# Moving a batch's projections up into the phase before, and finishing the last tokens tile by tile

## The chip, the cores and the metric

The kernel runs on one core of a Trainium2 chip. The metric is the device time in microseconds (us) of one execution; lower is better.

## The reference

Two layers on `x` of 4 batches, 512 tokens and 256 channels in float32, with a layer norm after each residual sum:

```python
x = layernorm(x + linear_attention(x))   # 16 heads of 128, elu(q)+1 and elu(k)+1, 4 key heads
x = layernorm(x + gated_update(x))       # 8 experts, the one with the largest gate, rank 8
x = layernorm(x + softmax_attention(x))  # 16 heads of 16, queries and keys from this x ("x2")
x = layernorm(x + top2_experts(x))       # 8 experts of 32, two by score, and a rank-16 part
```

In the softmax attention `q = x @ Wq`, `k = x @ Wk`, `v = x @ Wv`, and `softmax(q k / 4) v @ Wo` is taken per batch and head. In the expert layer the hidden vector (3 x 128 numbers for each token) is multiplied by a down matrix and added to `x`.

## The kernel before

Each engine has its own hand-written order of work; they meet only at semaphores. Tokens are cut into four tiles of 128 (`NT = 4`), the channels into two halves (`KD = 2`). Products that need accuracy are made in three passes of split numbers (`_hi` and `_lo`), so most results come as a pair: ScalarE (ACT) copies the `_hi` part out of PSUM, VectorE (DVE) subtracts to get the `_lo` part.

**First phase** (`layer0_attention`). Four batches, one after the other. For each, after keys and values, a run over 16 queries (`query(b, n)`), and then a run of 16 `project(b, n)`, which add into `bank_y`. Each project needs its head scaled: TensorE (PE) broadcasts a factor (`factor`), DVE multiplies (`scale`), ACT copies (`scaled_hi`), and the low part comes from DVE for even n and from GpSimd (POOL) for odd n (`scaled_lo`, lines 628 and 250). The factors of the second eight heads hang on `invert(b, 1)` (sum of the norms from `bank_n`, reciprocal) and `parts(b, 1)`. The norms' bank `bank_n` has no reader after that. In the last batch the function `beside(stage, n)` of each engine puts work of the second part between these steps: the gated update of batch 0 (`add_update`, `update_stats`, `merge`), its layer norm (`rstd` on POOL, `normalize` on ACT), the transpose of the result (`turn_x2` on PE, `x2T_out` on ACT, `x2T_rest` on DVE), `query_key(0, 0)`, and then, after the phase, `query_key(0, 1)`.

**Stack transfers.** The attention scores of layer 1 are products over 48 rows (16 channels as hi-hi, lo-hi and hi-lo). These rows are gathered by DMAs from `qk_hi` and `qk_lo` into `qs` and `ks` (`stack_rows`: two transfers of the hi part, one of the lo part). For batch 0 the query rows are issued by SP, the key rows by ACT.

**The lead.** After the first phase PE turns and selects batch 1 (`turn_x1`, `select`), makes half of the values (`value(0, 0)`), and then makes the scores of the first 8 heads (`LEAD = 8`), 32 products of 512 columns in four banks. For each, DVE takes a row maximum (`maxima`, line 1884). In between come the gate of batch 1 on DVE, `query_key(0, 2)` and `(0, 3)`, and `value(0, 1)`. Then four batches run through `body(b)`, 32 steps each.

**The end.** After the last body, PE, DVE and ACT work on the last two token tiles (t = 2, 3): transpose, route, `expert_up`, `expert_gate`, `hidden`, `turn_hidden_half`, `expert_out_half`, then add, layer norm and store. `keep_busy(home, count)` issues `count` matmuls of 512 columns whose result nobody reads; it waits until the bank `home` is free.

Banks of the second part lie on those of the first: `side` 0 and 1 on `bank_a`, name `"n"` on `bank_n`, `"s0"`, `"s1"`, `"st0"` on `bank_q`, `"c"` and `"t"` on `bank_y`.

Of the kernel before, what the change touches and what calls it, by code (L numbers as in the profile page):

```python
# [16 lines left out]
P = 128  # L17
# [115 lines left out]
def layer0_attention(nc, a, kept, ctx):  # L133

    with ExitStack() as memory:
# [431 lines left out]
        def vector(dve, beside):  # L567
# [105 lines left out]
            def body(b, last, more, beside=no_piece):  # L673
# [38 lines left out]
                query(b, 13)  # L712
                query(b, 14)
                scale(b, 2)
                scaled_lo(b, 2)
                query(b, 15)
                scale(b, 3)
                scale(b, 4)
                invert(b, 1)
# [50 lines left out]
def update_attention_experts(nc, a, kept, out, first):  # L770
# [6 lines left out]
    with ExitStack() as ctx:  # L777
# [65 lines left out]

        def by_k(home):
            return banks[home][:, :].rearrange("p (k n) -> p k n", k=KD)
# [24 lines left out]
        UP_AT, GATE_AT, HIDDEN_AT = ("s1", 0, 0, "st0"), ("s0", 1, 1, "st1"), ("c", "s0")  # L870
        lgT_half = x1T[0:E1, 1, 0:2 * P]
# [132 lines left out]
        def _(pool):  # L1004
# [67 lines left out]
            def beside(stage, n):  # L1072
# [8 lines left out]
                if stage == "scaled" and n == 7:  # L1081
                    rstd(2, 0)

            first.gpsimd(pool, beside)
            keep_x2(0)
# [19 lines left out]
        def _(pe):  # L1105
# [57 lines left out]
            def turn_x2(b, i):  # L1163
                turn(xf, x2T_done, x_ready[2], b, i, i)
                last_read[i] = (x2T_lo_ready, 2 * b + i + 1)

            def query_key(b, i):
# [3 lines left out]
                take(i % 2)  # L1171
# [3 lines left out]
                for k in range(KD):  # L1175
                    for lhs, rhs in split_passes(wqkv_hi[:, k, cols], wqkv_lo[:, k, cols], x2T_hi[:, k, :], x2T_lo[:, k, :]):
                        mm = pe.matmul(side[i % 2][:, :], lhs, rhs, start=n == 0, stop=n == 3 * KD - 1)  # L1177
                        n += 1
                mm.then_inc(qk_done, 1)
                last_read[i % 2] = (qk_lo_ready, 4 * b + i + 1)  # L1180
# [173 lines left out]

            def pair(b, n):
# [103 lines left out]
            def beside(stage, n):  # L1459
# [24 lines left out]
                if stage == "project":  # L1484
                    if n == 3:
                        take(0)
                    if n == 5:
                        take(1)
                    if n == 10:
                        last_read[0] = (first.m_lo_ready, maps + 7)  # L1490
                        turn_x2(0, 0)
                    if n == 12:
                        last_read[1] = (first.m_lo_ready, maps + 8)
                        turn_x2(0, 1)
                    if n == 14:
                        query_key(0, 0)

            first.tensor(pe, beside)
            query_key(0, 1)
# [33 lines left out]
            expert_out_half(last, 0)  # L1533
            turn_x3(last, 1, TURN_AT[1])
            route(last, 1, ROUTE_AT[1])
            turn_logits(last, 1, ROUTE_AT[1])
            for t in (2, 3):
                expert_up(last, t, UP_AT[t])
                expert_gate(last, t, GATE_AT[t])
            turn_hidden_half(last, 1)  # L1540
            expert_out_half(last, 1)

        @block.scalar
        def _(act):
# [27 lines left out]
            def x2T_out(b, i):  # L1572
# [4 lines left out]
                act.activation(x2T_hi[:, :, half_tokens(i)], side_k[i], ACT.Copy).then_inc(x2T_hi_ready, 1)  # L1577

            def qk_out(b, i):
                act.wait_ge(qk_done, 4 * b + i + 1)  # L1580
                at_least(act, stack_in[1 - i // 2], 16 * STACK_DMAS * (b + i // 2))
                act.activation(qk_hi[:, i % 2, :], side[i % 2][:, :], ACT.Copy).then_inc(qk_hi_ready, 1)
# [123 lines left out]
            def beside(stage, n):  # L1706
# [18 lines left out]
                if stage == "project":  # L1725
                    if n in (9, 10):
                        normalize(2, 0, xf, (0, 1) if n == 9 else (2, 3))
                    if n in (12, 14):
                        x2T_out(0, (n - 12) // 2)

            first.scalar(act, beside)
            for i in range(2):
                qk_out(0, i)
            stack_rows(act, 0, 1)
# [29 lines left out]
        def _(dve):  # L1764
# [104 lines left out]
            def x2T_rest(b, i):  # L1869
                dve.wait_ge(x2T_hi_ready, 2 * b + i + 1)  # L1870
                dve.tensor_tensor(x2T_lo[:, :, half_tokens(i)], side_k[i], x2T_hi[:, :, half_tokens(i)].bitcast(F32),
                                  ALU.subtract).then_inc(x2T_lo_ready, 1)

            def qk_rest(b, i):
                dve.wait_ge(qk_hi_ready, 4 * b + i + 1)
                dve.tensor_tensor(qk_lo[:, i % 2, :], side[i % 2][:, :], qk_hi[:, i % 2, :].bitcast(F32), ALU.subtract).then_inc(qk_lo_ready, 1)
# [245 lines left out]
            def beside(stage, n):  # L2122
# [8 lines left out]
                if stage == "query":  # L2131
# [9 lines left out]
                    if n == 11:  # L2141
                        add_update(0, 0)
                if stage == "project":
                    if n == 5:
                        add_update(0, 1)
                    if n == 6:
                        update_stats(0, range(NT))
                    if n == 7:
                        merge(2, 0)
                    if n in (13, 15):  # L2150
# [184 lines left out]
```

## Time and profile before

| | |
|---|---|
| median of 3 runs | 739.39 us (736.17 to 750.09) |
| the profiled execution | 738.66 us |
| its span, first to last instruction | 736.8 us |
| mean granted clock of TensorE | 0.968 of full speed |
| last project of the first phase starts | 333.57 us |
| first score of the lead starts | 347.32 us |
| first step of the bodies starts | 372.54 us |
| last `hidden` result starts | 722.75 us |

Times inside the trace count from the first instruction. A granted clock of 1.00 is TensorE's level of 2.4 GHz, 0.50 that of 1.2 GHz.

### The profile page before, as it was taken

What the parts mean: (1) busy time and instruction counts of PE and PEld (TensorE: products, weight loads), DVE (VectorE), ACT (ScalarE), POOL (GpSimd) and SP (SyncE); (2) the same over time, 40 slices, a digit from 0 to 9 for tenths busy, and PEclk for the clock granted to TensorE, in tenths of its full rate; (3) what the DMA queues carried; (4) which work ended last, traced back from release to release, by engine and by line L of the source; (5) the groups of instructions that cost most, each with busy time, mean ns of one, the idle gap of its engine ahead of it and who ended that gap; (6) DMA issues with size and microseconds to landing.
All of it is one profiled execution on the core that took longest, in us unless ns stands there. A gap on an engine that the chain in (4) does not pass through costs nothing.

```text
span 736.8 us, 11487 instructions
## 1 busy us (share of the span) xinstructions
PE 697.5 (95%) x4080; PEld 483.0 (66%) x4080; DVE 508.7 (69%) x1158; ACT 404.1 (55%) x745; POOL 106.1 (14%) x116
## 2 busy tenths in 40 slices
PE   8999999999999999997899998999999999999975
PEld 5768987798878887896544543555464555546654
DVE  4666556765577656774888797869779787783463
ACT  5574356643665377552137765766548566475531
POOL 0202320132103322232202000200001000000010
PEclk9999999999999999999789999999999999999996
DMA  8300000010000020005504600252004510000000
GB/s 337 149 1 1 29 1 1 0 47 0 0 0 0 12 79 1 4 1 87 123 4 76 99 3 0 41 91 45 2 1 78 90 37 2 2 1 30 1 30 28
DMA packets 13997, 28.31 MB, mean 38 GB/s; under 512 B 2612, under 2 KB 3452, under 8 KB 13820
## 3 DMA queue, kind: packets, MB, share of 16 engines
q1 hardware_dynamic: 13084, 26.10, 14.8%
q10 hardware_dynamic: 864, 1.57, 1.3%
q8 instruction: 29, 0.48, 0.3%
q14 instruction: 20, 0.16, 0.1%
HBM read 12.60 MB, written 2.10 MB: 20 GB/s over the span
## 4 chain that ended last, share of the span: by engine, by line
PE 68%; DVE 18%; issue 7%; ACT 2%; DMA 2%; POOL 1%; ACTq 0%; POOLq 0%; DVEq 0%; SPq 0%
PE bank_y L414 11%; PE bank_q L355 11%; PE bank_st L1231 8%; DVE nmax L1884 7%; PE bank_c L1244 6%; PE bank_a L298 5%; PE bank_a L385 3%; PE side L1177 3%; PE side L1298 2%; PE side L1329 2%; PE bank_a L332 2%; PE bank_n L370 2%; PE side L1191 2%; PE bank_q L397 2%; PE side L1264 2%
## 5 line engine op out<-in xcount | busy, mean ns | idle before, releaser
L1884 DVE TENSOR_REDUCE nmax<-bank_s 128x1 f32<-128x512 f32 x240 | 154.2, 684 | 54.8 <-PE bank_s L1208 53.5
L1597 ACT ACTIVATE shared<-bank_st 128x512 f32<-128x512 f32 x256 | 139.0, 596 | 66.6 <-PE bank_st L1231 65.7
L1208 PE MATMUL bank_s<-ks,qs 48*128 48x512 f32 x240 | 98.6, 472 | 5.9 <-DVE nmax L1884 3.9
L1231 PE MATMUL bank_st<-qs,ks 50*128 50x512 f32 x256 | 99.1, 457 | 3.5 <-ACT shared L1597 2.6
L617 DVE SCALAR_TENSOR_TENSOR sq<-bank_q,bq,eq 128x512 f32<-128x512 f32 x64 | 47.6, 744 | 48.2 <-ACT eq L500 48.2
L414 PE MATMUL bank_y<-m_hi,s_lo 128*128 128x256 f32 x256 | 73.3, 286 | 3.1 <-POOL s_lo L250 3.1
L414 PE MATMUL bank_y<-m_hi,s_hi 128*128 128x256 f32 x256 | 72.1, 282 | 0.0
L414 PE MATMUL bank_y<-m_lo,s_hi 128*128 128x256 f32 x256 | 72.1, 282 | 0.0
L1244 PE MATMUL bank_c<-shared,v 128*32 128x512 f32 x512 | 71.6, 633 | 0.0
L250 POOL TENSOR_TENSOR s_lo<-sq,s_hi 128x512 fp32r<-128x512 f32 x32 | 42.8, 1339 | 186.1 <-ACT s_hi L505 186.1
L1231 PEld LDWEIGHTS bank_st<-qs,ks 50*128 50x128 f32 x256 | 40.2, 186 | 40.8 <-issue 21.9
L505 ACT ACTIVATE s_hi<-sq 128x512 fp32r<-128x512 f32 x64 | 40.3, 631 | 44.2 <-DVE sq L634 44.2
L634 DVE TENSOR_TENSOR sq<-sq,bank_q 128x512 f32<-128x512 f32 x64 | 43.4, 684 | 23.4 <-PE bank_q L397 23.1
L498 ACT ACTIVATE eq<-bank_q,bq_neg 128x512 f32<-128x512 f32 x64 | 43.9, 686 | 26.0 <-PE bank_q L355 25.2
L355 PE MATMUL bank_q<-xT_hi,wq_lo 128*128 128x512 f32 x128 | 54.6, 427 | 1.3 <-DVE sq L617 1.3
L414 PEld LDWEIGHTS bank_y<-m_hi,s_lo 128*128 128x128 f32 x256 | 48.2, 188 | 5.8 <-issue 3.5
L355 PE MATMUL bank_q<-xT_hi,wq_hi 128*128 128x512 f32 x128 | 50.5, 394 | 0.0
L355 PE MATMUL bank_q<-xT_lo,wq_hi 128*128 128x512 f32 x128 | 50.4, 394 | 0.0
L1208 PEld LDWEIGHTS bank_s<-ks,qs 48*128 48x128 f32 x240 | 39.6, 189 | 16.3 <-DVE nmax L1884 13.7
L414 PEld LDWEIGHTS bank_y<-m_lo,s_hi 128*128 128x128 f32 x256 | 48.2, 188 | 0.2
L414 PEld LDWEIGHTS bank_y<-m_hi,s_hi 128*128 128x128 f32 x256 | 48.2, 188 | 0.0
L1029 POOL TENSOR_TENSOR ln_rstd<-ln_var,half 128x4 f32<-128x4 f32 (+1 forms) x12 | 11.5, 961 | 219.2 <-DVE ln_var L120 219.2
(282 smaller groups left out, 1370.3 us busy)
## 6 DMA issues: line engine op xcount, KB each, us to landing
qs<-qk_hi SPq DMA_DIRECT2D x16, 256.0 KB, 4.9
ks<-qk_hi SPq DMA_DIRECT2D x12, 256.0 KB, 7.1
xT<-in_xT SPq DMA_DIRECT2D x4, 512.0 KB, 4.5
sq<-in_wqT SPq DMA_DIRECT2D x2, 1024.0 KB, 9.2
wo<-in_woT SPq DMA_DIRECT2D x1, 2048.0 KB, 12.9
xs<-in_x SPq DMA_DIRECT2D x1, 2048.0 KB, 17.8
qs<-qk_lo SPq DMA_DIRECT2D x8, 256.0 KB, 5.5
ks<-qk_lo SPq DMA_DIRECT2D x6, 256.0 KB, 7.2
```

Of the source, the lines that this page charges most:

```text
L250: pool.tensor_tensor(s_lo[:, n % 3, :], sq[:, n, :], s_hi[:, n % 3, :].bitcast(F32), ALU.subtract).then_inc(s_lo_ready[1], 1)
L355: mm = pe.matmul(q_bank("query", n)[:, :], lhs, rhs, start=i == 0, stop=i == 3 * KD - 1)
L414: mm = pe.matmul(bank_y4[:, t, :], lhs, rhs, start=n == 0 and i == 0 and t % 2 == 0, stop=n == H0 - 1 and i == 2, skip_group_check=True)
L498: act.activation(eq[:, n % 3, :], q_bank("query", n)[:, :], ACT.Relu, bias=bq_neg[:, h:h + 1], scale=-1.0).then_inc(eq_capped, 1)
L505: act.activation(s_hi[:, n % 3, :], sq[:, n, :], ACT.Copy).then_inc(s_hi_ready, 1)
L617: dve.scalar_tensor_tensor(out=sq[:, n, :], in0=q_bank("query", n)[:, :], scalar=bq1[:, h:h + 1], in1=eq[:, n % 3, :], op0=ALU.add, op1=AL ...
L634: dve.tensor_tensor(sq[:, n, :], sq[:, n, :], q_bank("factor", n)[:, :], ALU.mult).then_inc(scaled, 1)
L1208: pe.matmul(score_bank(b, u)[:, :], qs[part, b % 2, slot, t * P:(t + 1) * P], ks[part, b % 2, slot, :], start=True, stop=True).then_inc(s_ ...
L1231: pe.matmul(bank_st[u % 2][:, :], ks[part, b % 2, slot, kt * P:(kt + 1) * P], qs[part, b % 2, slot, :], start=True, stop=True).then_inc(st ...
L1244: mm = pe.matmul(bank_c[32 * j:32 * j + 32, :], v[:, b % 2, kt, 4 * g + j, :], probs[:, (4 * s + j) % SLOTS, :], start=kt == 0, stop=kt == 3)
L1597: act.activation(probs[:, u % SLOTS, :], bank_st[u % 2][:, :], ACT.Exp, scale=SCALE1).then_inc(p_ready, 1)
L1884: dve.tensor_reduce(nmax[:, g, t, j:j + 1], score_bank(b, u)[:, :], AX.X, ALU.max, negate=True).then_inc(max_ready, 1)
```

## The change

1. DVE takes `add_update(0, 1)`, the statistics and `merge(2, 0)` of batch 0 earlier: beside queries 13, 14 and 15 and before `invert`, at `project` 4. The first phase gets four new places for `beside`, on DVE only.
2. POOL's `rstd(2, 0)` comes after `scaled_lo` 3 (7 before), its `keep_x2(0)` after `scaled_lo` 11 (before: after the phase). ACT's `normalize` goes from projects 9 and 10 to 5 and 6.
3. `turn_x2(0, 0)` and `(0, 1)` go to projects 6 and 8 (10 and 12 before), into `bank_n`; `query_key(0, 0)` to project 10 (14 before), into `bank_n`; `query_key(0, 1)` to project 11 (after the phase before), into `side` 0. Their copies, and ACT's DMAs of the first key rows, follow within the phase.
4. DVE: all of `normalize_x1(1)` at once; `gate_distances`, `gate_inverse` and `gate_scores` of batch 1 go from before the lead to behind the maxima of its head 0, `gate_largest(1)` behind head 2 and `gate_pick(1)` behind head 3.
5. The end: 18 more `keep_busy` matmuls in four groups, and the last two tiles are multiplied, added and measured one by one, in two banks.

```diff
@@ DVE, first phase (line 712)
                 query(b, 13)
+                beside("query", 13)
                 query(b, 14)
                 scale(b, 2)
+                beside("query", 14)
                 scaled_lo(b, 2)
                 query(b, 15)
+                beside("query", 15)
                 scale(b, 3)
                 scale(b, 4)
+                beside("project", 4)
                 invert(b, 1)
@@ banks
+        def x2_home(b, i):
+            return "n" if b == 0 else i
+        def qk_home(b, i):
+            return ("n", 0)[i] if b == 0 and i < 2 else i % 2
+        LAST_OUT_AT = {2: "s1", 3: "st0"}
@@ POOL
-                if stage == "scaled" and n == 7:
+                if stage == "scaled" and n == 3:
                     rstd(2, 0)
+                if stage == "scaled" and n == 11:
+                    keep_x2(0)
             first.gpsimd(pool, beside)
-            keep_x2(0)
@@ PE, beside, stage "project"
+                    if n == 6:
+                        last_read["n"] = (first.den_ready, 2 * B)
+                        turn_x2(0, 0)
+                    if n == 8:
+                        turn_x2(0, 1)
                     if n == 10:
+                        query_key(0, 0)
+                    if n == 11:
                         last_read[0] = (first.m_lo_ready, maps + 7)
-                        turn_x2(0, 0)
-                    if n == 12:
+                        query_key(0, 1)
                         last_read[1] = (first.m_lo_ready, maps + 8)
-                        turn_x2(0, 1)
-                    if n == 14:
-                        query_key(0, 0)
             first.tensor(pe, beside)
-            query_key(0, 1)
@@ PE, the end
+            def expert_out_last(t):
+                b, home = B - 1, LAST_OUT_AT[t]
+                pe.wait_ge(hidT_ready, 3 * b + 4)
+                take(home)
+                for c in range(3):
+                    mm = pe.matmul(by_k(home)[:, 0, :], hidT[:, c, t * P:(t + 1) * P], down1[:, c, :], start=c == 0, stop=c == 2)
+                mm.then_inc(down_done, 1)
...
             expert_out_half(last, 0)
+            keep_busy(0, 4)
             turn_x3(last, 1, TURN_AT[1])
+            keep_busy(0, 5)
             route(last, 1, ROUTE_AT[1])
...
+            keep_busy(1, 6)
             turn_hidden_half(last, 1)
-            expert_out_half(last, 1)
+            keep_busy(1, 3)
+            for t in (2, 3):
+                expert_out_last(t)
@@ ACT, beside, stage "project"
-                    if n in (9, 10):
-                        normalize(2, 0, xf, (0, 1) if n == 9 else (2, 3))
-                    if n in (12, 14):
-                        x2T_out(0, (n - 12) // 2)
+                    if n in (5, 6):
+                        normalize(2, 0, xf, (0, 1) if n == 5 else (2, 3))
+                    if n in (8, 10):
+                        x2T_out(0, (n - 8) // 2)
+                    if n in (12, 13):
+                        qk_out(0, n - 12)
+                    if n == 15:
+                        stack_rows(act, 0, 1)
             first.scalar(act, beside)
-            for i in range(2):
-                qk_out(0, i)
-            stack_rows(act, 0, 1)
@@ DVE, beside
+                    if n == 13:
+                        add_update(0, 1)
+                    if n in (14, 15):
+                        update_stats(0, (0, 1) if n == 14 else (2, 3))
                 if stage == "project":
-                    if n == 5:
-                        add_update(0, 1)
-                    if n == 6:
-                        update_stats(0, range(NT))
-                    if n == 7:
+                    if n == 4:
                         merge(2, 0)
-                    if n in (13, 15):
-                        x2T_rest(0, (n - 13) // 2)
+                    if n in (9, 11):
+                        x2T_rest(0, (n - 9) // 2)
+                    if n in (13, 14):
+                        qk_rest(0, n - 13)
@@ DVE, after the first phase
-            qk_rest(0, 0)
-            normalize_x1(1, (0, 1))
-            qk_rest(0, 1)
-            normalize_x1(1, (2, 3))
+            normalize_x1(1)
             residual(B - 1)
             for i in range(2):
                 projections(1, i)
-            gate_distances(1)
-            gate_inverse(1)
-            gate_scores(1)
             for h in range(LEAD):
                 maxima(0, h, range(NT))
                 if h == 0:
+                    gate_distances(1)
+                    gate_inverse(1)
+                    gate_scores(1)
+                if h == 2:
                     gate_largest(1)
-                if h == 1:
+                if h == 3:
                     gate_pick(1)
@@ DVE, the end
-            add_experts(last, 1, OUT_AT[1])
-            expert_stats(last, 1)
+            for t in (2, 3):
+                dve.wait_ge(down_done, 2 * last + t)
+                dve.tensor_tensor(xk[:, last % 2, t, :], by_k(LAST_OUT_AT[t])[:, 0, :], xk[:, last % 2, t, :], ALU.add).then_inc(r4_ready, 1)
+                dve.wait_ge(r4_ready, 2 * last + t)
+                tile_stats(4, xk[:, last % 2], (t,))
             merge(4, last, 1)
```

## Rows read from the trace of the kernel before

**Rows 1.** The page, part 1: busy time and share of the span.
```profile
PE 697.5 (95%) x4080; PEld 483.0 (66%) x4080; DVE 508.7 (69%) x1158; ACT 404.1 (55%) x745; POOL 106.1 (14%) x116
```

**Rows 2.** Windows: busy (instructions) of PE, PEld, DVE, ACT, POOL; clock; DMA share; GB/s.
```profile
336.90:347.30 10.40, 5.95 (x33) 5.44 (x33) 5.37 (x14) 3.57 (x12) 2.30 (x9) 0.84 0.82 129
358.70:368.70 10.00, 9.74 (x28) 6.32 (x28) 7.72 (x15) 1.18 (x2) 2.96 (x1) 0.51 0.39 104
375.70:382.20 6.50, 6.50 (x22) 2.38 (x20) 3.54 (x8) 1.56 (x4) 0.00 (x0) 0.51 0.01 3
723.50:730.10 6.60, 6.07 (x18) 4.57 (x16) 0.00 (x0) 0.87 (x2) 0.00 (x0) 0.50 0.11 40
```

**Rows 3.** Timeline of PE after the first phase: start, duration, line, [idle before <-releaser].
```profile
340.85 3.71 PE L1142 MATMUL side<-fw,x1T 128*128 128x136 f32 x16 [1.57 <-ACT x1T L1554]
...
347.32 0.70 PE L1208 MATMUL bank_s<-ks,qs 48*128 48x512 f32 x2 [1.28 <-DMA ks<-qk_lo]
```

**Rows 4.** The chain of waits, 330 to 380 us: start, duration, what.
```profile
333.73 1.45 PE bank_y L414 x12
335.18 1.41 PE side L1177 x6
...
339.45 7.73 DMA ks<-qk_lo
```

**Rows 5.** Timeline of ACT: last scaled head, first key-row DMAs, the copy behind them.
```profile
329.99 0.63 ACT L505 ACTIVATE s_hi<-sq 128x512 fp32r<-128x512 f32 x1 [0.36 <-DVE sq L634]
...
337.23 2.18 ACTq L925 DMA_DIRECT2D ks<-qk_hi  x2
...
340.11 1.09 ACT L1554 ACTIVATE x1T<-side 128x512 f32<-128x512 f32 x2 [2.91 <-PE side L1128]
```

**Rows 6.** Line 925, all stack transfers that SP issues: issue to landing.
```profile
DMA to landing us min/median/max: 4.4/5.5/8.9
```

**Rows 7.** Timeline of DVE, `invert(b, 1)` to the merge, and line 118 once more at 710.
```profile
306.47 0.42 DVE L639 TENSOR_SCALAR den<-bank_n 128x256 f32<-128x256 f32 x1 [0.79 <-PE bank_n L370]
...
310.13 0.86 DVE L1866 SCALAR_TENSOR_TENSOR xf<-xf,keep,side 128x256 f32<-128x256 f32 x2
...
312.11 1.39 DVE L1833 BATCH_NORM_STATS2 ln_bn<-xf 128x6 f32<-128x256 f32 x4
...
314.88 1.26 DVE L118 SCALAR_TENSOR_TENSOR ln_mean_neg<-ln_tmp,ln_bn 128x4 f32<-128x4 f32 x1
...
710.03 0.16 DVE L118 SCALAR_TENSOR_TENSOR ln_mean_neg<-ln_tmp,ln_bn 128x2 f32<-128x2 f32 x1
```

**Rows 8.** Timeline of POOL: two of the odd low parts, and `keep_x2(0)`.
```profile
305.82 1.28 POOL L250 TENSOR_TENSOR s_lo<-sq,s_hi 128x512 fp32r<-128x512 f32 x1 [5.43 <-ACT s_hi L505]
...
314.84 1.29 POOL L250 TENSOR_TENSOR s_lo<-sq,s_hi 128x512 fp32r<-128x512 f32 x1 [2.98 <-ACT s_hi L505]
...
331.94 2.43 POOL L1051 TENSOR_TENSOR xs<-xf,bo 128x1024 f32<-128x1024 f32 x1
```

**Rows 9.** The page, part 5: all 64 queries on DVE, busy, mean ns, idle before.
```profile
L617 DVE SCALAR_TENSOR_TENSOR sq<-bank_q,bq,eq 128x512 f32<-128x512 f32 x64 | 47.6, 744 | 48.2 <-ACT eq L500 48.2
```

**Rows 10.** Timeline of PE: project 5 and its wait.
```profile
312.00 0.36 PE L414 MATMUL bank_y<-m_hi,s_lo 128*128 128x256 f32 x1 [0.31 <-POOL s_lo L250]
```

**Rows 11.** Windows, columns as in rows 2: the gate of batch 1, first part.
```profile
345.05:347.35 2.30, 1.02 (x10) 0.85 (x8) 2.05 (x8) 0.60 (x1) 0.00 (x0) 1.00 0.07 12
```

**Rows 12.** Timeline of DVE: the lead's one long gap.
```profile
368.12 1.29 DVE L1884 TENSOR_REDUCE nmax<-bank_s 128x1 f32<-128x512 f32 x2 [2.21 <-PE bank_s L1208]
```

**Rows 13.** Timeline of PE and DVE, the end.
```profile
708.05 2.75 PE L1351 MATMUL bank_s<-down,turned 128*128 128x256 f32 x12
...
725.17 5.35 PE L1351 MATMUL bank_s<-down,turned 128*128 128x256 f32 x12 [0.54 <-ACT turned L1631]
...
730.55 0.69 DVE L1990 TENSOR_TENSOR xk<-bank_s,xk 128x512 f32<-128x512 f32 x1 [7.38 <-PE bank_s L1351]
731.28 0.75 DVE L1833 BATCH_NORM_STATS2 ln_bn<-xk 128x6 f32<-128x256 f32 x2
```

More of the change, by code:

```diff
@@ L1163, in turn_x2 @@
             def turn_x2(b, i):
-                turn(xf, x2T_done, x_ready[2], b, i, i)
-                last_read[i] = (x2T_lo_ready, 2 * b + i + 1)
+                turn(xf, x2T_done, x_ready[2], b, i, x2_home(b, i))
+                last_read[x2_home(b, i)] = (x2T_lo_ready, 2 * b + i + 1)
             def query_key(b, i):
@@ L1170, in query_key @@
                 pe.wait_ge(x2T_lo_ready, 2 * (b + 1))
-                take(i % 2)
+                home = qk_home(b, i)
+                take(home)
                 first = (i % 2) * D + (i // 2) * P
@@ L1176, in query_key @@
                     for lhs, rhs in split_passes(wqkv_hi[:, k, cols], wqkv_lo[:, k, cols], x2T_hi[:, k, :], x2T_lo[:, k, :]):
-                        mm = pe.matmul(side[i % 2][:, :], lhs, rhs, start=n == 0, stop=n == 3 * KD - 1)
+                        mm = pe.matmul(banks[home][:, :], lhs, rhs, start=n == 0, stop=n == 3 * KD - 1)
                         n += 1
                 mm.then_inc(qk_done, 1)
-                last_read[i % 2] = (qk_lo_ready, 4 * b + i + 1)
+                last_read[home] = (qk_lo_ready, 4 * b + i + 1)
             def value(b, i):
@@ L1353, in expert_out_half @@
                 last_read[OUT_AT[i]] = (r4_ready, 2 * b + i + 1)
+            def expert_out_last(t):
+                b, home = B - 1, LAST_OUT_AT[t]
+                pe.wait_ge(hidT_ready, 3 * b + 4)
+                take(home)
+                for c in range(3):
+                    mm = pe.matmul(by_k(home)[:, 0, :], hidT[:, c, t * P:(t + 1) * P], down1[:, c, :], start=c == 0, stop=c == 2)
+                mm.then_inc(down_done, 1)
             def pair(b, n):
@@ L1576, in x2T_out @@
                     act.wait_ge(first.sk_sum_step, (NT - 1) * B)
-                act.activation(x2T_hi[:, :, half_tokens(i)], side_k[i], ACT.Copy).then_inc(x2T_hi_ready, 1)
+                act.activation(x2T_hi[:, :, half_tokens(i)], by_k(x2_home(b, i)), ACT.Copy).then_inc(x2T_hi_ready, 1)
             def qk_out(b, i):
@@ L1581, in qk_out @@
                 at_least(act, stack_in[1 - i // 2], 16 * STACK_DMAS * (b + i // 2))
-                act.activation(qk_hi[:, i % 2, :], side[i % 2][:, :], ACT.Copy).then_inc(qk_hi_ready, 1)
+                act.activation(qk_hi[:, i % 2, :], banks[qk_home(b, i)][:, :], ACT.Copy).then_inc(qk_hi_ready, 1)
             def value_out(b, i):
@@ L1870, in x2T_rest @@
                 dve.wait_ge(x2T_hi_ready, 2 * b + i + 1)
-                dve.tensor_tensor(x2T_lo[:, :, half_tokens(i)], side_k[i], x2T_hi[:, :, half_tokens(i)].bitcast(F32),
+                dve.tensor_tensor(x2T_lo[:, :, half_tokens(i)], by_k(x2_home(b, i)), x2T_hi[:, :, half_tokens(i)].bitcast(F32),
                                   ALU.subtract).then_inc(x2T_lo_ready, 1)
@@ L1875, in qk_rest @@
                 dve.wait_ge(qk_hi_ready, 4 * b + i + 1)
[L1876 removed]
+                dve.tensor_tensor(qk_lo[:, i % 2, :], banks[qk_home(b, i)][:, :], qk_hi[:, i % 2, :].bitcast(F32), ALU.subtract).then_inc(qk_lo_ready, 1)
             def maxima(b, h, ts):
```

## The prediction, made before the changed kernel ran

> **What bounds the kernel now.** I read the page's first part first: PE is busy 95% of the span, DVE 69% [rows 1], so only stretches where PE idles, waits or runs at half clock can give much. Windows along the span show such stretches, the timeline of PE shows what lies in them, and the chain of waits what ends each wait.
>
> There are two, and the change touches both. Between the first phase and the first score (336.9 to 347.3) PE is busy 5.95 of 10.40 us at a mean clock of 0.84, so 3.3 us of it pass at the lower level, 1.2 GHz [rows 2]. The chain goes there through ACT's DMA issues and the last key rows' transfer, 339.45 to 347.18 [rows 4]; PE's first score waited 1.28 us for it, so PE alone was ready at 346.04 [rows 3]. The transfer is the later of two close ends, and moving it alone would give 1.3 us. From there DVE is the bound, 32 maxima with small work between, until the bodies start at 372.54; its one long gap is 2.21 us [rows 12]. After that PE bounds again.
>
> The second stretch is the end: the last 12 matmuls take 5.35 us at a clock of 0.50, where 12 equal ones at 708 take 2.75, and DVE waits 7.38 us [rows 2, 13].
>
> **The norm step moved ahead of invert.** DVE loses, between 310.1 and 316.3, the update (0.8), four statistics (1.3) and the merge (1.7, of which one instruction of 4 columns took 1.26) [rows 7]: 3.8 us. Update and statistics go behind queries 13 to 15, where DVE waits for ACT's exponential, 0.75 us in the mean of 64 [rows 9]. They hold 0.8, 0.7 and 0.7 us, so they fit, and DVE comes free near 306.4, as the norms are ready. Cost 0; if the gaps close, up to 0.8. The merge does stand in the way: DVE works in order, and behind it are invert, low part 4 and scale 5. I cost it 1.0 us: 0.7 of its own, and a wait until POOL's low part ends at 307.10 [rows 8]. Project 4 is then 0.4 late; project 5, which already waits 0.31 us for POOL's low part [rows 10], is 1.0 late, and 0.2 comes back at project 6 through the lighter DVE. Bounds 0 (the merge fits into the 0.79 us wait for the norms [rows 7]) and 1.0; I take 0.8, the nearer, since the chain runs through DVE there.
>
> **The moved PE, ACT and POOL work.** A project takes 1.45 us, a query_key 1.41 [rows 4]; moving changes neither, and PE has no gap from project 7 on. PE ends with project 15 and both query_keys at 336.6 + 0.8 = 337.4. It waits for no new neighbour: x2 is normalized by 315 while project 6 ends at 317, each x2T copy has a project or more before its reader, and bank_n is read out by 309.5. ACT's copies stand between scaled heads of which PE has two in hand; POOL's keep_x2 (2.43 us) [rows 8] fits between its low parts 11 and 13, which two query_keys spread. Cost 0; where such cover is gone, 0.4 to 0.7 each.
>
> What comes earlier is transfers. SP's three go out near 328.3, not 334.4. ACT's three follow scaled_hi 15, now at 329.99 [rows 5]; that head's factor moves behind two query_keys, 2.8 + 0.8 us, so ACT issues at 334.2 instead of 337.23 and the last one at 336.4 instead of 339.45. It took 7.73 us with five others in flight [rows 4]; stack transfers of the whole run take 4.4 to 8.9, median 5.5 [rows 6]. So it lands between 340.8 and 345.3; I take the median, as only its two fellows are in flight: 341.9.
>
> PE's own path: turn_x1 at 337.4, no longer behind DVE's normalization. ACT's x1T copy came at 340.11 as its DMA issues stood ahead [rows 5]; they now end at 337.0, the copy comes at 337.9, and select at 338.6 instead of 340.85. Select and the half values took 5.2 us (340.85 to 346.04), 3.3 of them at half clock [rows 2, 3]; at full clock 3.6. The clock fell at 341.4, after PE had worked 0.7 of 3.9 us; its gap there is now 0.3, so I take full clock, ready at 342.2 (at the old mix 343.8). First score: the later of 341.9 and 342.2, plus 0.1, so 342.3: 5.0 earlier (bounds 2.0 and 5.2).
>
> **The gate in the lead.** The gate's first part, 345.07 to 347.33 [rows 11], ran while DVE waited for the first score. Now it stands behind the first four maxima, where DVE bounds: its full 2.26 us. On ACT gate_exp waits for it, and behind gate_exp are queued the copies of query_keys 2 and 3, win_hi and the second key-row DMAs; they have 2 us in hand, since DVE takes those low parts only after heads 1 and 2. The rest of the gate changes places only. Bodies start 5.0 - 2.3 = 2.7 us earlier. Bounds: 0.3 later (landing at 345.3) and 4.0 earlier (values (0, 1), behind which DVE's gap of 2.21 lies, at full clock: 1.1 more, with landing early).
>
> **The end.** Its critical run is DVE's routing and hidden, until 723.17. The first nine keep_busy matmuls stand in PE waits of 1.3 and 1.4 us, six more follow the experts (721.4) and take 1.4 at full clock; all fit. At half they push by up to 0.5, which goes into the range. If the clock is full at 723, transposes end at 724.05 instead of 724.6, three keep_busy end at 724.85, the 12 matmuls take 2.75 (727.6), and of add and statistics one tile's half, 0.85, remains: 728.45, against 732.03 now [rows 13]. That is -3.6. If it is half, keep_busy ends at 725.9, the matmuls at 731.25, the statistics at 732.1: +0.1. I take full clock by the nearer row: at 708.05 PE held it behind work with gaps no longer than the 1.5 and 0.7 us that remain.
>
> **Sum**, against the profiled execution (738.66: its span of 736.8 and 1.9 around it; 0.7 below the median of the three runs): 738.66 - 2.7 - 3.6 = **732.4**.
>
> **A rule against the change.** DVE's instruction of 4 columns that took 1.26 us ended at 316.14, POOL's low part at 316.13; the same line took 0.16 us with POOL idle [rows 7, 8]. The Trainium skill, page "SBUF — State Buffer", section "Who interferes with whom", says that a DVE instruction with two SBUF inputs contends with a GpSimd instruction that reads SBUF, and one blocks for the other's whole length. By that rule, the trace agrees in this pair, and keep_x2, moved into the phase, can hold low part 12. The sum would be 733.1 (rival 5) instead of 732.4.
>
> **The rivals.**
> 1. *keep_busy doesn't hold the clock.* The end gives +0.1: 738.66 - 2.7 + 0.1 = 736.1. For it: the clock fell twice between 716 and 724, behind routing matmuls of 8 output columns and behind a gap of 1.9 us. Against: 18 full matmuls are put in. 20%.
> 2. *The key rows land late*, at 345.3: transition +0.3, end -3.6, 735.4. For it: the DMA is the later end now [rows 3]. Against: three transfers in flight, not six. 10%.
> 3. *The clock turns against the kernel* (slower than before). Ten us at half clock lie in the lead, where DVE bounds and they cost little; 6.5 lie in the first body, where PE is always busy [rows 2]. If the ten slide into the body they cost half, 5.0; with half clock at the end too, 738.66 - 2.7 + 0.1 + 5.0 = 741.1. It decides from 5.2 us more at half clock in the body than now. 10%.
> 4. *The clock turns in its favour*: the body's 6.5 us go (3.3) and the values run at full clock (1.1): 732.4 - 4.4 = 728.0. 13%.
> 5. *keep_x2 holds DVE.* Low part 12 then ends at 331.6 at the latest instead of 329.2; project 12 wants it near 330.9: +0.7, 733.1. 5%.
> 6. My forecast, 732.4: 42%.
>
> **How the numbers follow.** The range 727.5 to 739.5 holds all cases but the third: 0.5 beyond the fastest, and 3.4 beyond the slowest of the others for a late landing joined with rival 1 (+3.0) and a late route (0.5). Two per cent, about what a measurement of this kernel can tell from no change, is 14.8 us: 724.6 to 754.2. No case reaches either end: faster would take 3.4 us more than rival 4 (3%), slower 13 us beyond rival 3 (2%); within 95%.
>
> **What would show each step.** Right: invert about 1 us later and project 5 late; ACT's first ks DMA near 334; x1T near 338, select under 2 us; first score near 342.3 behind a transfer of 4.4 to 6 us; 2.3 us of gate work behind the first four maxima; bodies from 369.8; granted clock 1.00 under the last 12 matmuls and 2.75 us for them. Wrong: a first score after 345, a clock of 0.50 under the last matmuls, or a PE wait for x2T or bank_n within the projects. It fails most easily by the clock, which no edit sets directly.

## The result, and the profile after

| | before | changed |
|---|---|---|
| median of 20 runs | 740.94 us (736.17 to 750.27) | 734.64 us (729.96 to 830.44) |
| ratio, 95% interval | | 0.9898 [0.9868, 0.9928] |
| profiled execution, its span | 738.66, 736.8 | 734.44, 732.6 |
| mean granted clock | 0.968 | 0.968 |

The time lies in the range, 2.2 us above the predicted 732.4, and within 2% of before. The gain is real: the interval leaves out 1. Ratios and their intervals leave out every execution more than 1.5% above the fastest of its kernel (here three of each twenty, and five of the twelve of experiment 7), while medians are of all.

The page, part 1, of the changed kernel: the shares are within 1% of those of before [rows 1], with 18 matmuls more.
```profile
PE 700.4 (96%) x4098; PEld 482.7 (66%) x4098; DVE 509.8 (70%) x1159; ACT 403.2 (55%) x745; POOL 105.9 (14%) x116
```

**The transition.** The timeline of PE in the changed kernel, answering to [rows 3, 10]: project 5, transposes, select, the last values product and the first scores.
```profile
313.18 0.36 PE L414 MATMUL bank_y<-m_hi,s_lo 128*128 128x256 f32 x1 [0.77 <-POOL s_lo L250]
...
337.43 1.04 PE L1141 MATMUL side<-ident,xf 128*128 128x128 f32 x8
338.81 2.09 PE L1155 MATMUL side<-fw,x1T 128*128 128x136 f32 x16 [0.34 <-ACT x1T L1584]
...
342.04 0.28 PE L1205 MATMUL side<-wqkv_hi,x2T_hi 128*128 128x256 f32 x1
342.25 0.73 PE L1222 MATMUL bank_s<-ks,qs 48*128 48x512 f32 x2
```
The first score carries no wait. Select and the values take 3.44 us (338.81 to 342.25), 5.2 before. The timeline of ACT, answering to [rows 5], says why the copy before select is early: the DMA issues are over at 335.7.
```profile
333.75 1.31 ACTq L937 DMA_DIRECT2D ks<-qk_hi  x2
335.10 0.61 ACTq L937 DMA_DIRECT2D ks<-qk_lo  x1
338.07 1.08 ACT L1584 ACTIVATE x1T<-side 128x512 f32<-128x512 f32 x2 [3.69 <-PE side L1141]
```
Windows of the changed kernel, columns as in [rows 2]: the transition at full clock, the gate inside the lead, then two stretches at the lower level, one in the lead and one over the start of the bodies.
```profile
336.90:342.30 5.40, 5.06 (x43) 4.72 (x42) 2.11 (x3) 2.67 (x10) 2.30 (x9) 1.00 0.49 64
345.19:347.45 2.26, 2.26 (x10) 1.49 (x9) 2.06 (x10) 0.00 (x0) 0.00 (x0) 1.00 0.00 0
350.00:365.00 15.00, 12.26 (x32) 7.09 (x33) 12.93 (x30) 1.18 (x2) 4.00 (x5) 0.54 0.74 144
367.00:385.00 18.00, 17.90 (x54) 7.40 (x54) 12.22 (x25) 5.43 (x10) 0.00 (x0) 0.53 0.01 1
```
DVE around `invert`, answering to [rows 7], and the lead's long gap, answering to [rows 12] (1.76 us instead of 2.21):
```profile
306.23 1.25 DVE L118 SCALAR_TENSOR_TENSOR ln_mean_neg<-ln_tmp,ln_bn 128x4 f32<-128x4 f32 x1
...
307.67 0.42 DVE L639 TENSOR_SCALAR den<-bank_n 128x256 f32<-128x256 f32 x1
...
364.77 1.29 DVE L1915 TENSOR_REDUCE nmax<-bank_s 128x1 f32<-128x512 f32 x2 [1.76 <-PE bank_s L1222]
```
and POOL's low part beside it, answering to [rows 8]: DVE's instruction of 4 columns ends at 307.48, POOL's at 307.46.
```profile
306.19 1.27 POOL L250 TENSOR_TENSOR s_lo<-sq,s_hi 128x512 fp32r<-128x512 f32 x1 [6.07 <-ACT s_hi L505]
```

**The end.** Timeline of PE and of DVE in the changed kernel, answering to [rows 13]:
```profile
720.38 1.64 PE L1130 MATMUL side<-x2T_hi,wqkv_hi 128*128 128x512 f32 x6 [1.39 <-DVE sg L1968]
...
723.05 0.94 PE L1130 MATMUL side<-x2T_hi,wqkv_hi 128*128 128x512 f32 x3
724.04 1.56 PE L1375 MATMUL bank_s<-down,turned 128*128 128x256 f32 x6
725.44 1.46 PE L1375 MATMUL bank_st<-down,turned 128*128 128x256 f32 x6
```
```profile
725.64 0.42 DVE L2228 TENSOR_TENSOR xk<-bank_s,xk 128x256 f32<-128x256 f32 x1 [3.27 <-PE bank_s L1375]
...
727.39 0.43 DVE L1864 BATCH_NORM_STATS2 ln_bn<-xk 128x6 f32<-128x256 f32 x1
```
The 12 matmuls take 2.86 us, not 5.35, and DVE has added and measured the first tile before the second is ready.

**Where the time goes.** Four marks, read from the timelines, cut each span: N, the start of the last 16 norm matmuls (line 370); the first score; the first step of the bodies; and the last `turn_context`, where the bodies end. Three of the moved DVE pieces (the update and the statistics beside queries 13 to 15) run before N, but they don't move it: from the 16 norm matmuls before these to N it is 9.19 to 9.21 us in all fourteen traces. All profiled executions of this study in one table, in us; the column "low clock" is the part of the bodies in which the trace records a granted clock of 0.50:

| execution | N | N to first score | N to bodies | bodies | low clock | end | span |
|---|---|---|---|---|---|---|---|
| before | 305.33 | 41.99 | 67.21 | 332.02 | 17.1 | 32.24 | 736.8 |
| before, again | 304.19 | 41.75 | 66.88 | 332.48 | 18.4 | 30.45 | 734.0 |
| end only | 303.90 | 41.97 | 68.50 | 333.04 | 20.3 | 28.86 | 734.3 |
| keep_busy only | 304.37 | 41.97 | 67.06 | 336.08 | 29.2 | 29.39 | 736.9 |
| tiles only | 304.16 | 41.96 | 68.49 | 333.00 | 20.3 | 28.85 | 734.5 |
| changed | 305.04 | 37.21 | 64.37 | 334.36 | 25.5 | 28.83 | 732.6 |
| changed, again | 304.61 | 37.20 | 65.79 | 337.57 | 30.5 | 28.83 | 736.8 |
| front only | 304.39 | 37.22 | 65.80 | 333.82 | 23.1 | 30.39 | 734.4 |
| gate before the lead | 305.15 | 37.20 | 64.42 | 334.69 | 25.5 | 28.84 | 733.1 |
| merge behind scale 5 | 304.82 | 35.98 | 63.25 | 334.99 | 23.9 | 28.84 | 731.9 |
| keep_busy in the lead | 304.93 | 37.20 | 70.78 | 334.83 | 26.0 | 28.86 | 739.4 |
| keys after the phase | 304.85 | 41.03 | 69.59 | 330.30 | 13.2 | 28.86 | 733.6 |
| values at head 3 | 304.10 | 37.16 | 63.96 | 333.79 | 21.6 | 28.85 | 730.7 |
| three edits | 305.32 | 36.03 | 61.46 | 334.65 | 25.4 | 28.87 | 730.3 |

Between the two profiled executions the span falls by 4.20: N -0.29, N to bodies -2.84, bodies +2.34, end -3.41. The sum forecast -6.3; what is missing are the 2.34 us of the bodies, in which no instruction was changed. What the table shows beside that: N to first score repeats within 0.02 in most rows, N to bodies has two values 1.4 us apart for the same order of work, and the bodies take anything from 330.3 to 337.6.

The length of the bodies goes with the low clock in them. A straight line through the fourteen rows gives 0.37 us for each us at the lower level, and no row is over 0.8 us from it. Between the two profiled executions there are 8.4 us more at the lower level; the line makes 3.1 us of them, and 2.34 were measured.

### The profile page after: what moved, and what is told of

Read it like the earlier page. It is cut to its first block, busy times and chain, and to the rows that moved or that the text cites. A ratio compares the mean times of both kernels' runs of the same rounds, so it can differ in the third digit from the quotient of the medians.

```text
span 732.6 us, 11524 instructions
## 1 busy us (share of the span) xinstructions
PE 700.4 (96%) x4098; PEld 482.7 (66%) x4098; DVE 509.8 (70%) x1159; ACT 403.2 (55%) x745; POOL 105.9 (14%) x116
## 4 chain that ended last, share of the span: by engine, by line
PE 70%; DVE 18%; issue 7%; ACT 3%; POOL 1%; DMA 1%; DVEq 0%; POOLq 0%; SPq 0%; ACTq 0%
PE bank_y L414 11%; PE bank_q L355 10%; PE bank_st L1245 8%; DVE nmax L1915 7%; PE bank_c L1258 6%; PE bank_a L298 5%; PE bank_a L385 3%; PE side L1191 2%; PE side L1312 2%; PE side L1343 2%; PE bank_a L332 2%; PE side L1205 2%; PE side L1278 2%; PE bank_n L370 2%; PE bank_q L397 2%
## 5 line engine op out<-in xcount | busy, mean ns | idle before, releaser
L1222 PE MATMUL bank_s<-ks,qs 48*128 48x512 f32 x240 | 100.6, 481 | 4.7 <-DVE nmax L1915 3.9
L1245 PE MATMUL bank_st<-qs,ks 50*128 50x512 f32 x256 | 101.1, 465 | 2.1 <-ACT shared L1627 1.3
```

The costliest lines, as they stand in the source:

```text
L1222: pe.matmul(score_bank(b, u)[:, :], qs[part, b % 2, slot, t * P:(t + 1) * P], ks[part, b % 2, slot, :], start=True, stop=True).then_inc(s_ ...
L1245: pe.matmul(bank_st[u % 2][:, :], ks[part, b % 2, slot, kt * P:(kt + 1) * P], qs[part, b % 2, slot, :], start=True, stop=True).then_inc(st ...
```

## The experiments

Two series undo the change by halves; the next take single terms of the sum apart; the last repeat both kernels and try a better one. Ratios are to the kernel before, on the same chip, in the same session.

**1. Front only.** The changed kernel with the end of before:
```diff
-            keep_busy(0, 4)
...
-            keep_busy(1, 3)
-            for t in (2, 3):
-                expert_out_last(t)
+            expert_out_half(last, 1)
```


> The changed kernel with the old end: edits 1 to 4 alone. Theory: the bodies start 3 us earlier than 372.54 (near 369.5), and that stays: 736.2 to 738 where the kernel before takes 740.9. Rival (only the clock moved): the earlier start is eaten by half clock in the first body, as in the changed kernel's profile, where 3.1 us at the start of the bodies are 0.8 us at their end; then this kernel is within 1 us of the one before, and the changed kernel's gain is the end's alone.

Measured: median 737.83, before 743.21 in the same session; 0.9966 [0.9925, 1.0007]. The interval holds 1. In the trace the first score comes 37.22 after N, as in the changed kernel, and the bodies take 333.82.

**2 to 4. End only, keep_busy only, tiles only.** The kernel before with both parts of the new end, with the 18 `keep_busy` matmuls alone, or with `expert_out_last` and the tile-wise add and statistics alone:
```diff
             expert_out_half(last, 0)
+            keep_busy(0, 4)
             turn_x3(last, 1, TURN_AT[1])
+            keep_busy(0, 5)
...
+            keep_busy(1, 6)
             turn_hidden_half(last, 1)
+            keep_busy(1, 3)
```
```diff
-            expert_out_half(last, 1)
+            for t in (2, 3):
+                expert_out_last(t)
```


> The kernel before with the new end alone (18 keep_busy matmuls and the last two tiles one by one). Theory: from the last hidden to the end 3.5 us less than before (before: 722.75 to 736.8, so 14.1 us; here 10.6), 3.4 to 3.6 us off the time. Rival: under 1 us, because the clock held there by chance in the one profile seen.

> The kernel before with the 18 keep_busy matmuls alone; the last two tiles still added as one half. If the clock carries the gain: granted clock 1.00 under the last 12 matmuls, 2.75 us for them, and last hidden to end 11.3 us, so 2.8 us off. If the tile by tile order carries it: nothing or 0.5 slower.

> The kernel before with the last two tiles one by one and no keep_busy. If the clock carries the gain: 12 matmuls at half clock in 5.35 us, and only one tile's add and statistics saved, 0.6 us, last hidden to end 13.4 us. If the order carries it: 2 us or more.

Measured: medians 738.40, 742.03 and 738.94; ratios 0.9959 [0.9909, 1.0009], 0.9982 [0.9941, 1.0023] and 0.9975 [0.9926, 1.0025]. Every interval holds 1, so the times alone settle nothing. Their middle values, 0.4% for the whole end and 0.3% for the front, make up most of the 0.9 to 1.0% of the whole, but none of them is told from nothing. The traces say more. The end of the kernel before, in its second execution (timelines of PE and DVE):
```profile
724.84 2.86 PE L1351 MATMUL bank_s<-down,turned 128*128 128x256 f32 x12 [0.74 <-ACT turned L1631]
```
```profile
727.73 0.69 DVE L1990 TENSOR_TENSOR xk<-bank_s,xk 128x512 f32<-128x512 f32 x1 [4.57 <-PE bank_s L1351]
728.46 0.75 DVE L1833 BATCH_NORM_STATS2 ln_bn<-xk 128x6 f32<-128x256 f32 x2
```
The same 12 matmuls, with no `keep_busy` ahead of them, at full clock: 2.86 us where [rows 13] have 5.35. The expectation for tiles only had counted on 5.35 again; it took 2.86 as well. The lower level was there too, but earlier. Windows over the last experts' matmuls and over the last products, of that execution:
```profile
714.00:721.00 7.00, 6.54 (x27) 6.42 (x27) 4.43 (x23) 0.98 (x3) 0.65 (x2) 0.53 0.01 2
723.50:728.50 5.00, 3.45 (x18) 2.55 (x16) 0.73 (x2) 0.87 (x2) 0.00 (x0) 1.00 0.14 52
```
of front only, and of tiles only:
```profile
714.00:721.00 7.00, 6.54 (x28) 6.09 (x27) 4.22 (x23) 0.97 (x3) 0.89 (x2) 0.51 0.01 2
```
```profile
714.00:721.00 7.00, 5.32 (x27) 4.88 (x28) 4.68 (x26) 1.42 (x4) 0.89 (x2) 0.76 0.01 2
```
and of end only, with `keep_busy`:
```profile
714.00:721.00 7.00, 5.94 (x38) 4.70 (x36) 4.68 (x26) 1.50 (x6) 0.89 (x2) 1.00 0.01 2
723.50:728.50 5.00, 4.55 (x22) 3.29 (x21) 1.28 (x4) 0.87 (x2) 0.00 (x0) 1.00 0.03 10
```
All four executions without `keep_busy` pass some of the end at 1.2 GHz, and what that costs hangs on where it falls: 2.8 us over the last transposes and products, 2.5 of them on the last 12 matmuls (before: 32.24), 1.0 on the experts' matmuls, which DVE waits for (30.45, 30.39), nothing between 717 and 721 (tiles only: 28.85). All nine executions with `keep_busy` and tiles end in 28.83 to 28.87 us, and with keep_busy only, the tenth, the clock is full under these matmuls too. So `keep_busy` does what it was put in for, and takes away a loss of 0 to 2.8 us. The tiles are worth 0.54 at full clock (29.39 without, 28.85 with them).

**5. Gate before the lead.** The changed kernel, with the gate's first part where it was:
```diff
+            gate_distances(1)
+            gate_inverse(1)
+            gate_scores(1)
             for h in range(LEAD):
                 maxima(0, h, range(NT))
-                if h == 0:
-                    gate_distances(1)
-                    gate_inverse(1)
-                    gate_scores(1)
```


> The changed kernel with gate_distances, gate_inverse and gate_scores of batch 1 before the lead again. DVE has 1.4 us idle there, between its last projection (341.4) and the first maximum (342.79), the gate takes 2.26: theory, the first maximum comes 0.9 us later, the bodies start 1.4 us earlier (368.1 instead of 369.5). Rival: the gate was moved because it would hold the first maxima, so the bodies start later or the same.

Measured: median 735.06, before 740.43; 0.9950 [0.9907, 0.9992]. The first maximum starts 0.79 later after N (38.54, was 37.75), and `value(0, 1)` at 360.20 instead of 361.47. Yet the bodies start where they did, at 369.57. The window from `value(0, 1)` to the bodies has the reason: PE is always busy, at half clock, and needs 9.4 us; in the changed kernel it needed 7.9, with full clock from 364.15 to 367.56.
```profile
360.10:369.60 9.50, 9.50 (x30) 6.36 (x29) 6.62 (x11) 1.19 (x2) 0.54 (x1) 0.50 0.23 77
```
In the changed kernel's first execution (PE alone; then clock, DMA share and GB/s):
```profile
364.85:365.70 0.85, 0.85 (x6) 1.00 0.14 38
```
The same stretch of its second execution was at half clock, as in this experiment:
```profile
361.00:370.00 9.00, 9.00 (x28) 6.29 (x27) 6.41 (x11) 1.19 (x2) 0.46 (x1) 0.50 0.27 81
```
These are the two values of "N to bodies": 64.37 with full clock in the lead's last heads, 65.79 and 65.80 without. Against those, this kernel's 64.42 is 1.4 us less. So the gate inside the lead costs its 2.26 us there and spares 0.79 in front: this part of edit 4 is a loss, of 1.47 by this sum and of 1.4 as measured, but that shows only among executions with the same clock. In the pair of first profiles the clock took all of it back.

**6. Merge behind scale 5.** The changed kernel, with DVE's `merge(2, 0)` after `invert`, low part 4 and scale 5, and `rstd` and `normalize` one step later with it:
```diff
-                beside("project", 4)
                 invert(b, 1)
...
                     scale(b, n)
+                    if n == 5:
+                        beside("project", 4)
```


> The changed kernel with the merge behind scale 5 instead of before invert, rstd on POOL behind its low part 5, normalize on ACT at projects 6 and 7. Theory: the merge before invert is what makes project 5 start at 313.2 instead of 312.0; here it starts near 312.0 and the first score 0.8 to 1.2 us earlier (near 341.3), the bodies as much. Rival: the first phase loses nothing to the merge, the times stay.

Measured: median 733.73; 0.9957 [0.9923, 0.9992]. `invert` starts 1.14 after N (changed kernel: 2.63, before: 1.14), the first score comes 1.23 earlier and the bodies 1.12. Timeline of DVE, the instruction that had taken 1.25 us, now clear of POOL's low parts:
```profile
309.50 0.17 DVE L118 SCALAR_TENSOR_TENSOR ln_mean_neg<-ln_tmp,ln_bn 128x4 f32<-128x4 f32 x1
```
So 1.2 us of the transition were lost to the place of five instructions of 4 columns (`rstd` and `normalize` moved with them, as they wait for them).

**7. keep_busy in the lead.** Twelve of these matmuls between the scores of heads 2 to 7, to hold the clock over the start of the bodies:
```diff
+            pe.wait_ge(first.res_ready, B)
...
                     score(0, h, t)
+                    if h > 1 and t in (1, 3):
+                        keep_busy("c", 1)
```


> The changed kernel with 12 more keep_busy matmuls in the lead (two per head from head 2 on, in PE's waits for DVE). Theory: they fill PE where it waits and hold its clock; half clock in the lead and first body, 350.5 to 384.5 in the changed kernel's profile, gets shorter by 10 us or more, and the time falls by 2 to 6 us. Rival: PE's work there delays the scores for DVE, 12 x 0.23 to 0.43 us, and the bodies start up to 3 us later without a better clock.

Measured: median 734.26, 727.71 to 749.41, with six of twelve executions at 730.4 or less and six from 738 to 749; 0.9858 [0.9811, 0.9906]. Its profile was taken in one of the longer executions (741.22), and serves only to show what happened there: PE never idle, and half clock all the same.
```profile
360.00:370.00 10.00, 10.00 (x26) 5.94 (x27) 5.60 (x9) 1.06 (x2) 1.77 (x1) 0.50 0.23 74
```
The bodies began 5.0 us later after N than in the changed kernel's second execution; the added matmuls at half clock, which stand in the way of the scores, would explain it. In the six shorter executions, four of them under 729, the clock was higher: their mean granted clock is 0.983 to 0.987, that of the six longer ones 0.949 to 0.968, and no execution of the changed kernel has over 0.978. As far as time and mean clock go, the theory came true in half of the executions and the rival in the other half. In which stretch the clock was gained stays open, since no profile shows a short execution. The ratio is that of seven executions; the medians of all, 734.26 and 740.43, differ by 0.8%, and the changed kernel's own median is as low.

**8. Keys after the phase.** The changed kernel with `query_key(0, 1)`, its copies and ACT's key-row DMAs back behind the phase:
```diff
-                        query_key(0, 1)
...
             first.tensor(pe, beside)
+            query_key(0, 1)
...
             first.scalar(act, beside)
+            qk_out(0, 1)
+            stack_rows(act, 0, 1)
...
             normalize_x1(1)
+            qk_rest(0, 1)
```


> The changed kernel with query_key(0, 1), its copies and ACT's key-row transfers behind the first phase again; all else changed. PE's own work to the first score is the same, so if PE's path is the bound (my forecast) nothing moves, and if the key rows' landing becomes the bound, the first score comes near 344.7 (last transfer issued at 339.2 and 5.5 us in flight) instead of 342.3, and the bodies 2.4 us later.

Measured: median 737.37; 0.9952 [0.9907, 0.9997]; first score 3.82 later, bodies 3.8 later than at the same clock. PE's timeline and the chain of waits:
```profile
338.88 1.07 PE L1141 MATMUL side<-ident,xf 128*128 128x128 f32 x8 [1.50 <-DVE qk_lo L1907]
...
345.88 0.70 PE L1222 MATMUL bank_s<-ks,qs 48*128 48x512 f32 x2 [1.58 <-DMA ks<-qk_lo]
```
```profile
339.39 6.36 DMA ks<-qk_lo
```
The transfer ends last again, 1.58 us after PE. But PE's own path is late too: the transposes share bank `side` 0 and wait 1.50 us for DVE's low part. The expectation that PE's own work stays the same was wrong. Of the 3.82 us the transfer makes 1.58 and PE's path 2.24, so moving the keys up paid twice, for the transfer and for the bank. The span shows little of it, since in this profile the bodies take only 330.3, with the least low clock of all rows, 13.2 us. The other five executions about as short have the same mean granted clock, 0.974 or 0.975.

**9, 10. Both kernels again,** unchanged, to see how much an execution differs from the next.

> The changed kernel once more, beside the next two. Last hidden to end 10.2 us as in every kernel with keep_busy; bodies start near 369.5; 6 to 7.5 us below the kernel before.

> The kernel before once more, for its own spread and a second profile of its end. If half clock under the last 12 matmuls belongs to the kernel, they take 5.35 us again and last hidden to end is 13.6 us. If it depends on where a half-clock stretch falls, as the front-only kernel suggests (old end, yet 10.8 us), it can as well be 10.8. Ratio 1.00 either way.

Measured: changed 734.97, before 741.09 in the same session, 0.9914 [0.9878, 0.9951]; the kernel before against itself 741.21, 1.0019 [0.9983, 1.0056]. The profiles are in the table: the second of the changed kernel is 4.2 us longer than the first, the second of before 2.8 shorter.

Each execution's mean granted clock is on record, and the time goes with it. Of the kernel before there are 110 executions with a clock, in three sessions: 32 are over 745 us, at 0.942 to 0.956, and 9 under 735, at 0.969 to 0.978. Their median clock is 0.961; that of 30 executions of the changed kernel (without the one of 830.44 us, at 0.74) is 0.968. Part of this difference is the change's own: after the bodies the two traces of before have 10.0 and 13.4 us at the lower level, those of the changed kernel 1.4 and 3.2.

**11, 12. A better version.** In the lead `value(0, 1)`, 12 matmuls, stands in front of head 6 and makes DVE's gap of 1.76 us. Experiment 11 makes it after head 3; experiment 12 joins this with experiments 5 and 6.
```diff
+                if h == 3:
+                    value(0, 1)
                 if h == 4:
                     turn_max(0, 0)
-                if h == 5:
-                    value(0, 1)
```


> The changed kernel with value(0, 1) behind the scores of head 3 instead of head 5. Theory: from head 6 on the lead is bound by PE at half clock, behind these 12 matmuls (2.83 us); at head 3 PE waits for DVE anyway, so DVE's gap of 1.8 us before head 6 goes and the bodies start 1.5 to 2 us earlier, near 367.7. Rival: they push turn_max and with it the first shift transfer, and the bodies start no earlier.

> The changed kernel with three edits: merge behind scale 5 (first score 1.4 us earlier), the gate's first part before the lead (1.3 us earlier at head 5), value(0, 1) at head 3 (1.5 to 2). Theory: bodies start near 365.5 and the time is 3 to 4 us below the changed kernel's, if the bodies have no more half clock than there. Rival: a third or more goes to half clock in the bodies, and the gain is under 2 us.

Measured: median 734.10 and 0.9914 [0.9878, 0.9949]; median 731.14 (729.49 to 735.57, and one execution of 1252.65) and 0.9891 [0.9837, 0.9944]. Both ran with the lead's last heads at half clock, so they stand against 65.80: the values save 1.84 us, the three together 4.34, which is just 1.38 + 1.12 + 1.84. By its median the joined kernel beats the changed one by 3.8 us (734.97 in that session) and the one before by 10, but its interval, from six runs, overlaps with the changed kernel's. Up to the start of the bodies its gain is shown; in the whole time it is likely, not shown.

## Why the prediction came out as it did

It was right in sign, in size and in most steps, and its two large terms were there in the profile. Its 2.0 us between sum and profiled execution (732.4, 734.44) come from a term that it had as rivals only. Some of the agreement is luck. The medians differ by 6.3 us, exactly the forecast gain, but the 3.6 of the end in it held against one execution only, and the steps shown apart, 2.7 to 2.8 for the transition and 2.2 for the end, make about 5.0.

- **Transition, -2.7.** At equal clock in the lead's last heads it measured -2.84 (67.21 to 64.37) and -2.70 (68.50 to 65.80). Right.
- **First score at 342.3.** It came at 342.25, but N lay 0.29 earlier; counted from N the gain was 4.78, not 5.0. Issue of the key rows at 333.75 (forecast 334.2), last one at 335.10 (336.4), copy at 338.07 (337.9), select at 338.81 (338.6), at full clock as argued. The last key rows landed at 341.24 (341.9), 1.0 before the score. In the kernel before the clock fell at 341.12, not at 341.4; that changes nothing in the sum. Experiment 8 confirms that the transfer ends last when it isn't moved.
- **The merge, +0.8 on PE.** Mis-sized: 1.2 at the first score by experiment 6. `invert` was 1.49 late and project 5 1.47, where the step had 1.0. The step named the cause, a DVE instruction held until POOL's low part ends, but had that end too early: at 307.10, 1.77 after N, as in the kernel before. It came at 307.46, 2.42 after N. The reason lies one term ahead, "Cost 0" for the update and the statistics. DVE waits for ACT's exponential ahead of a query, and behind query 15 no query follows. DVE before, then changed:
```profile
304.40 1.27 DVE L634 TENSOR_TENSOR sq<-sq,bank_q 128x512 f32<-128x512 f32 x2
```
```profile
304.12 0.74 DVE L1864 BATCH_NORM_STATS2 ln_bn<-xf 128x6 f32<-128x256 f32 x2
304.77 1.27 DVE L634 TENSOR_TENSOR sq<-sq,bank_q 128x512 f32<-128x512 f32 x2
```
  The statistics hold `scale(b, 3)`, which starts 0.27 before N and no longer 0.93, and through ACT's copy POOL's low part is 0.65 late as well. In experiment 6, where the statistics stay behind query 15, this low part ends 2.42 after N too, and project 4 starts 0.64 and project 5 0.17 later after N than before.
- **The gate, 2.26 in the lead.** Its duration was exactly that (345.19 to 347.45). From the first score to the bodies the change cost 1.94 (25.22 to 27.16) or, in the other clock, 2.05 (26.53 to 28.58), so the term was 0.2 to 0.3 too large, and the term of the first score as much too large: they cancel.
- **The rule of the Trainium skill** ("SBUF — State Buffer", section "Who interferes with whom"), that a DVE instruction with two SBUF inputs contends with a GpSimd instruction that reads SBUF: the trace agrees once more, 1.25 us beside POOL and 0.17 without. The delay of `keep_x2`'s neighbours that rival 5 feared didn't occur: POOL ran it from 325.37 to 327.80, and low part 12 was on time. No DVE instruction with two such inputs was due then, so this isn't a test of the rule.
- **Rivals 1, 2 and 4** didn't occur. `keep_busy` held the clock in all ten traces. The first key rows were no end any more: issued by 335.7, and no transfer of that stretch took over 6.1 us. The clock was not in favour in either profile of the changed kernel. Of its first 20 executions five look like rival 4: 729.96 to 731.41 us, with a mean granted clock of 0.974 to 0.978, where the profiled one has 0.968.
- **The end, -3.6.** -3.41 against the profiled execution, right there. As a gain of the average execution the step fails, and its agreement with the profile is luck: it took one execution's half clock for the rule. Over the three executions with the old end the mean is 31.03, so the change gives 2.2, of which 0.54 is from the tiles.
- **Rival 3, the clock.** It happened in part: the stretch at the lower level that lay in the lead before [rows 2] reached over the start of the bodies, to 385, where before 6.5 us lay in the first body. Over all the bodies 17.1 us were at the lower level before and 25.5 after, and the bodies took 2.34 longer. The rival counted half of such time as lost; by the line through the table it is 0.37. The larger share of low clock isn't shown to be a consequence of the change: the bodies of the old front took 332.0 to 336.1 and those of the new one 330.3 to 337.6. The means, 333.3 of five and 334.3 of nine, differ by less than either spread.

The medians differ by 6.3 us and the profiled executions by 4.2, because the median of before lies 2.3 above its profiled execution, that of the changed kernel 0.2. The clocks on record go with that: the profiled execution of before had 0.968, where the median of its executions is 0.961, and the changed kernel's had 0.968, its median. What stays open is where in the longer executions of before the low clock lies, which no profile shows, and how much of the difference in clock is the change's. And why the clock falls in the lead and the first body while PE is 82 to 100% busy there wasn't settled.

## What to carry to other kernels

Measure a step from the last mark that the edit doesn't move, and compare executions whose clock is the same in the stretch: gains of 1.1 to 1.8 us, lost in spans that scatter by 4, then repeat to 0.1 and add up. Before small work is put in front of a serial step, ask what POOL does at that moment; the same five instructions cost 1.2 us more or nothing by their place. A place is free only if the engine waits behind it: a wait ahead of the last query covered nothing put behind it. And a loss by a low clock that one profile shows at one place is a sample, so take at least a second profile of the kernel before, and compare the mean clock of the profiled execution with that of the others, before the sum counts on its return.

## What the hardware showed that was not expected

- The clock stayed low with PE busy without a gap: 9.50 of 9.50 us and 10.00 of 10.00 us at 0.50 in the lead (experiments 5 and 7). It also fell so: in the changed kernel it rose at 364.15 and fell at 367.56, with gaps of 0.17 us in all between, and PE was busy 17.90 of 18.00 us from 367 to 385, at 0.53.
- Over the bodies a us at the lower level came with 0.37 us more time, less than the 0.5 that rival 3 took.
- Where the lower level falls changes from one execution of a kernel to the next: in the old end it cost 2.8, 1.0, 1.0 and 0 us. The Trainium skill, page "TensorE: Matmul & The Clock Gate", Part 1, says that the same kernel measures different numbers of matmuls at the lower clock from run to run, and puts the penalty of the ramp, the matmuls before the clock first rises, under 1% of a typical span. The traces agree with the first. The second speaks of the ramp alone; in mid-kernel the bodies spread by 7.3 us over executions, 1.0% of 735, and that is as large as the whole change.
- One DVE instruction of 4 columns (line 118) took 1.25 or 1.26 us in all twelve traces that have the merge in the place of the kernel before or of the changed one, and 0.17 in the two that have it elsewhere. A delay by a neighbour on POOL is as repeatable as the instruction's own time.
- The stretch up to N, on which the edits have no effect that shows, took 303.90 to 305.33 us.
